# A four-layer mixture-of-experts network on one Trainium2 core: where a pair's last residues and the next pair's input split stand on VectorE

## The reference, cut to what matters

```
x = x + _L0_ffn_ref(_L0_cond_ref(x, cond_8, ...), ...)    # gated MLP chosen per batch, attention over 16 experts
x = x + _L1_ffn_ref(_L1_cond_ref(x, cond_8, ...), ...)
# _L1_ffn_ref, x here is the output h of the conditioned layer:
shared = relu(xt @ sW1 + sb1) @ sW2 + sb2                 # the shared expert, every token
probs = softmax(xt @ router_W + router_b)
top_p, top_i = top_k(probs, 3)                            # 3 of 15 routed experts per token
routed = sum_e cw[n, e] * (relu(xt @ eW1[e] + eb1[e]) @ eW2[e] + eb2[e])
return shared + routed
```

## Time and profile before

| what | value |
|---|---|
| time, median of 3 runs (lowest to highest) | 1533.56 us (1532.3 to 1539.36) |
| the profiled execution: its own time, its span | 1535.98 us, 1534.1 us |
| TensorE busy | 1321.8 us, 86% |
| VectorE, ScalarE, GpSimd busy | 1030.5 us (67%), 591.7 us (39%), 701.5 us (46%) |
| mean granted TensorE clock | 0.898 |
| chain that ended last, by engine | PE 56%, DVE 16%, issue 10%, POOL 9%, ACT 4% |

### The profile page before, as it was taken

How to read it: one execution, slowest core, us unless ns; L and a number is a source line. 1 busy time by engine, 2 the same in 40 slices (tenths; PEclk the granted TensorE clock), 3 DMA queues, 4 the chain that set the end, 5 groups by cost and what they waited for, 6 DMA issues and landing times.

```text
span 1534.1 us, 18711 instructions
## 1 busy us (share of the span) xinstructions
PE 1321.8 (86%) x6536; PEld 1118.3 (73%) x6536; DVE 1030.5 (67%) x1854; ACT 591.7 (39%) x984; POOL 701.5 (46%) x371
## 2 busy tenths in 40 slices
PE   5999989999994799727888999988898979896698
PEld 4898776898782799715776788876687767774587
DVE  8499665499753555526766433498648884789887
ACT  3302422301420588604445455534552445342241
POOL 4320113720015467573002453386656674467790
PEclk9898987898985899958999999999999999996798
DMA  5300001400006699841000332221121222121000
GB/s 197 133 29 14 28 28 55 139 26 3 1 14 226 206 280 310 266 156 55 1 0 21 107 106 89 76 82 63 62 90 55 76 82 85 41 69 47 9 1 28
DMA packets 51773, 128.74 MB, mean 84 GB/s; under 512 B 6353, under 2 KB 30433, under 8 KB 51553
## 3 DMA queue, kind: packets, MB, share of 16 engines
q1 hardware_dynamic: 43840, 109.86, 22.0%
q0 software_dynamic: 4608, 12.59, 2.5%
q10 hardware_dynamic: 3232, 5.11, 0.9%
HBM read 105.25 MB, written 22.28 MB: 83 GB/s over the span
## 4 chain that ended last, share of the span: by engine, by line
PE 56%; DVE 16%; issue 10%; POOL 9%; ACT 4%; DMA 2%; another core or an unknown queue 2%; ACTq 1%; SPq 0%; POOLq 0%; DVEq 0%
PE bank L405 17%; PE bank L408 16%; PE bank L409 16%; POOL VW L458 4%; DVE bank L2335 2%; DVE G L458 1%; PE bank L804 1%; POOL w_lo L593 1%; DVE acc L2359 1%; DVE F L2359 1%; DVE acc L2628 1%; PE bank L953 1%; PE bank L774 1%; ACT w_hi L1601 1%
## 5 line engine op out<-in xcount | busy, mean ns | idle before, releaser
L405 PE MATMUL bank<-x_hi,w_hi 128*128 128x512 f32 (+1 forms) x560 | 221.6, 396 | 38.5 <-POOL w_lo L636 16.3
L636 POOL TENSOR_TENSOR w_lo<-raw,w_hi 128x1024 fp32r<-128x1024 f32 x48 | 117.7, 2453 | 226.5 <-ACT w_hi L1601 211.7
L408 PE MATMUL bank<-x_lo,w_hi 128*128 128x512 f32 (+1 forms) x560 | 215.4, 385 | 0.0
L409 PE MATMUL bank<-x_hi,w_lo 128*128 128x512 f32 (+1 forms) x560 | 214.6, 383 | 0.0
L405 PEld LDWEIGHTS bank<-x_hi,w_hi 128*128 128x128 f32 x560 | 111.8, 200 | 65.6 <-POOL w_lo L636 20.1
L405 PE MATMUL bank<-hid_hi,w_hi 128*128 128x512 f32 x328 | 134.3, 409 | 27.3 <-DVE hid_lo L2290 12.8
L1707 ACT ACTIVATE hid_hi<-bank 128x512 fp32r<-128x512 f32 x96 | 57.4, 598 | 196.4 <-DVE bank L2335 196.4
L409 PE MATMUL bank<-hid_hi,w_lo 128*128 128x512 f32 x328 | 131.8, 402 | 0.0
L408 PE MATMUL bank<-hid_lo,w_hi 128*128 128x512 f32 x328 | 131.8, 402 | 0.0
L409 PEld LDWEIGHTS bank<-x_hi,w_lo 128*128 128x128 f32 x560 | 111.5, 199 | 19.9
L408 PEld LDWEIGHTS bank<-x_lo,w_hi 128*128 128x128 f32 x560 | 111.9, 200 | 18.5
(11 more groups left out here) (473 smaller groups left out, 3643.6 us busy)
## 6 DMA issues: line engine op xcount, KB each, us to landing
raw<-in_skill SPq DMA_DIRECT2D x32, 768.0 KB
raw<-in_shared SPq DMA_DIRECT2D x16, 768.0 KB
raw<-in_l1e SPq DMA_DIRECT2D x20, 513.0 KB
base<-xs SPq DMA_DIRECT2D x38, 256.0 KB, 4.5
ys<-F SPq DMA_DIRECT2D x38, 256.0 KB, 5.0
VW<-in_l1e SPq DMA_DIRECT2D x18, 513.0 KB, 5.2
raw<-in_l0c SPq DMA_DIRECT2D x12, 512.0 KB
raw<-in_qkv SPq DMA_DIRECT2D x8, 768.0 KB
```

What stands on the lines that cost most here:

```text
L405: i = nc.tensor.matmul(out, sh, mh, start=first, stop=False)
L408: nc.tensor.matmul(out, sh, ml, start=False, stop=False)
L409: return nc.tensor.matmul(out, sl, mh, start=False, stop=last)
L636: nc.gpsimd.tensor_tensor(lo[:, UP3], src[:, UP3], hi[:, UP3].bitcast(F32), ALU.subtract).then_inc(w_up_ready.sem, 1)
```

## The change

On VectorE, the four residues of the shared expert stand between `place_rows(0)` and `place_rows(1)`, in both pairs. In pair 0, the split of the next pair's `xT[2]` follows them, and that of `xT[3]` follows `place_rows(1)`; at the head of pair 1 there is no split any more. On TensorE, pair 1 waits for `sh_done` of pair 0 as well, since `x_pair` no longer says that the banks are free.

```
@@ TensorE, head of a pair
                         if cc == 0:
                             pe.wait_ge(*x_pair(it, u + 1))
+                            if it > 0:
+                                pe.wait_ge(*sh_done(it - 1, u + 1))
@@ VectorE
-                def split_x(layer, u):
-                    step(v.tensor_copy(x_hi[u][:], xT[2 * it + u][:]))
-                    v.tensor_tensor(x_lo[u][:], xT[2 * it + u][:], x_hi[u][:].bitcast(F32),
+                def split_x(batch, u):
+                    step(v.tensor_copy(x_hi[u][:], xT[batch + u][:]))
+                    v.tensor_tensor(x_lo[u][:], xT[batch + u][:], x_hi[u][:].bitcast(F32),
                                     ALU.subtract).then_inc(x_pair.sem, 1)

-                dve.wait_ge(*x_in[2 * it](0, 1))
-                split_x(0, 0)
                 if it == 0:
+                    dve.wait_ge(*x_in[0](0, 1))
+                    split_x(0, 0)
                     prepare_gates()
-                dve.wait_ge(*x_in[2 * it + 1](0, 1))
-                split_x(0, 1)
+                    dve.wait_ge(*x_in[1](0, 1))
+                    split_x(0, 1)
@@ the two calls in the middle: split_x(1, u) becomes split_x(2 * it, u)
...
@@ VectorE, end of a pair
                 place_rows(0)
-                place_rows(1)
                 for u in U:
                     for m in range(KD):
                         dve.wait_ge(*sh_hi(it, 2 * u + m + 1))
                         v.tensor_tensor(hid_lo[u][:, m, :], B(u, m)[:], hid_hi[u][:, m, :].bitcast(F32),
                                         ALU.subtract).then_inc(sh_lo.sem, 1)
+                if it == 0:
+                    dve.wait_ge(*x_in[2](0, 1))
+                    split_x(2, 0)
+                place_rows(1)
+                if it == 0:
+                    dve.wait_ge(*x_in[3](0, 1))
+                    split_x(2, 1)
```

More of the change, by code:

```diff
@@ L2024, in _ @@
                     if n == 13:
-                        split_x(1, 0)
+                        split_x(2 * it, 0)
                 projected(1, 0)
@@ L2028, in _ @@
                 wbot_residue(1)
-                split_x(1, 1)
+                split_x(2 * it, 1)
                 RE = slice(1, E1)
```

## The result

The changed kernel takes 1514.95 us (median of 4 runs) beside 1532.93 us for the kernel before (4 runs): a ratio of 0.9898, 95% interval 0.9851 to 0.9945. The same two kernels compared again in two later groups of runs, on chips of their own, gave 0.9924 (0.9896 to 0.9952) and 0.9931 (0.9911 to 0.9951). Taken from the ratios the gain is 10.4 to 15.6 us, by the medians 12.3 to 18.0 us, against 14.7 forecast. One of the four runs of the changed kernel, 1696.72 us with a mean granted TensorE clock of 0.717, is left out of the ratio, as are single runs of 4783.94 and 2529.63 us in the later groups.

The account below looks back on a forecast made before the run. The kernel was taken as bound by TensorE (56% of the chain), with waits on other engines. 4.40 + 3.56 + 1.30 us in pair 0 and 4.40 + 1.08 in pair 1 make 14.74: 1518.8 us, range 1512.5 to 1526.

Parts of the forecast that it names:

- The residues in pair 0: End of pair 0: TensorE's whole stall before the first down matmul goes, 4.40 us.
- named as a sign: In the changed kernel's profile, the stall before the first down matmul is below 0.5 us in both pairs.
- The split and the added wait: Pair 0's end: stall before next pair's first matmul goes, 3.56 us; splits hidden, wait for `sh_done` priced at 0.
- The clock in pair 0: Down straight behind `rank(1)` takes 7.17 us instead of 8.47: 1.30 us less, bounds 0 and 2.97.
- The HAM clock gate: Skill's rule: closing an idle gap leaves the clock high, down takes 5.50 us, sum 3.3 us larger over both pairs.
- The whole stretch from ranks to head: End of pair 0's `rank(1)` to next pair's first matmul: 4.40, 3.56 and 1.30 us less.
- Pair 1: End of pair 1: 4.40 us stall and 1.08 us of down's time gained, 5.48 us passed on through ScalarE's train.
- rival B: Pair 1: delays of ScalarE's copies vanish, falling before the densest DMA traffic; 5.3 us more, 1513.5 us; 11%.
- rival D: ScalarE's zeroing train, pair 1: all seven DMAs go slow, train 14.8 us longer, 1533.6 to 1536 us; 5%.
- Rival A: Pair 1's gain is not passed on, as ScalarE's and SP's zeroing trains overlap; 1524.3 to 1521.9 us; 20%.
- Rival C: Clock terms are 0 or negative, the fall reaching into the next pair's head; 1524.4 to 1521.2 us; 14%.
- The sum: Both pairs: 14.74 us gained, from a median of 1533.56 to 1518.8 us.

Follow-up runs that it names:

- first group: On one chip, against the kernel before: residues alone 1521.52 us, split alone 1530.03, changed kernel with pair 1 in old order 1525.65, changed kernel again 1519.93.
- late scatters: Kernel before plus eight idle GpSimd subtractions between pair 1's last twelve scatters: 1514.69 us, with the kernel before at 1508.47.
- other trains: Kernel before with twelve zeroing DMAs issued from SP and three from ScalarE: 1509.92 us, ratio 1.0004.
- third group: On one chip, ratios to the kernel before: itself 1.0001, changed kernel 0.9931, kernel before with `ZERO_SP = 12` 1.0004, changed kernel with early `rank(0)` 0.9938.
- second and third group: Second: idle GpSimd work in changed kernel 1498.47 us, in kernel before 1514.69; changed kernel with `ZERO_SP = 5` 1498.88, also with early `rank(0)` 1497.4. Third: see its line.

## Why the prediction was right, and where it was not

**The residues in pair 0: right.** Forecast 4.40 us. In the changed kernel's first profile no wait is left, with the residues alone 0.21 us, and in its repeats 0.53 and 0.33 us: a gain of 3.9 to 4.4. 0.53 is just over the 0.5 us that I had named as a sign. I had put VectorE's free moment 4.4 us ahead of the end of `rank(1)`; it was 2.6 us ahead in the first profile and 0.8 us in the one with 0.53.

**The split and the added wait: right.** Forecast 3.56 us hidden; the split alone gave 3.59. Nothing waits for `sh_done`: head follows the bias matmuls without idle in every profile that has the split moved.

**The clock in pair 0: right in the mean, and in three executions of seven.** I took one row, 7.17 us for down. In seven executions with the residues early and `rank(0)` in its old place it took, up to the first transpose, 5.59, 6.86, 8.46, 8.39, 5.57, 7.12 and 7.03 us, a mean of 7.00; in the old order it took 8.26 to 8.31 in five. (The prediction's 8.47 and 7.17 end 0.16 us later, with the last matmul.) The windows of the changed kernel show both levels of the clock (2.4 GHz throughout, then mostly 1.2 GHz):

```profile
221.00:228.00 7.00, 7.00 (x39) 5.79 (x40) 6.52 (x18) 0.18 (x2) 4.01 (x4) 1.00 0.21 75
443.00:452.00 9.00, 9.00 (x29) 7.33 (x30) 7.80 (x25) 0.00 (x0) 5.51 (x6) 0.63 0.41 139
```

TensorE is busy all of the time in both. The rule of the Trainium skill weighed in the prediction ("TensorE: Matmul & The Clock Gate", The HAM clock gate) fits the first and not the second, so neither it nor my row alone could have said 5.6 here and 8.3 there. A closed gap gave back between nothing and 2.7 us of clock.

What I had not looked at is where the clock fell. Stretches of pair 0, one of the changed kernel's first profile and two of its repeat in the first group:

```profile
214.30:217.60 3.30, 3.30 (x10) 2.62 (x10) 2.80 (x16) 0.35 (x1) 0.00 (x0) 0.50 0.00 0
```

```profile
214.00:223.00 9.00, 9.00 (x68) 8.43 (x67) 7.70 (x42) 4.62 (x9) 0.78 (x1) 1.00 0.19 58
223.50:230.00 6.50, 5.97 (x15) 4.67 (x15) 6.05 (x18) 0.00 (x0) 4.66 (x4) 0.50 0.21 76
```

In the first the clock fell in `rank(0)`'s 128x16 matmuls (211.12 to 214.4), the low level lay under `shared_up(1)`, and down ran at the high one. In the second it was high all through `shared_up(1)` and fell at the end of `rank(1)`'s 128x16 matmuls (223.54), so the low level lay under down. Of the seven executions two are of the first kind (5.59 and 5.57 us) and five of the second (6.86 to 8.46). In the kernel before it fell behind both. So part of what down shows as gained or lost is only the low stretch moved by one block; and where `shared_up(1)` ran at the high level, TensorE came to down sooner against VectorE, which fits the waits of 0.21 to 0.53 us that are left in four of those five. My 7.17 us stands for the second kind: with its measure three of the five took 7.02, 7.28 and 7.20 us.

The whole stretch from ranks to head was forecast 9.26 us shorter. It was 21.68 to 21.75 us in four executions of the kernel before (one with late scatters, one with other trains), and 14.14, 14.16, 12.26, 11.86, 11.25 and 11.25 in six of the new order: 7.5 to 10.5 us less, 9.2 in the mean. That the mean meets the forecast is partly luck: the two executions with the clock high throughout down and the two with it low for some 6 us of it lie about as far off on either side.

**Pair 1: the step that failed.** I wrote that "ScalarE's start sets the end" and let 5.48 us through, with the scatters "some 10 us of slack". In the first profile of before the start was indeed on the path. In the changed kernel ScalarE's train starts 10.4 us after the ranks instead of 20.7, 4.40 us of it by the stall and the rest by rival B, the copies' delays, which went; the clock gave nothing (down 8.28 us against 8.25). But then something else ends the stretch. In the changed kernel's first profile it is the last scatter's landing, 2.5 us behind SP's issue train. In its repeat and with the residues alone it is SP's own train, at 0.7 us a step, which SP left without any wait for a DMA. At the quick pace it is the scatters again. The term is 7.7 and 9.7 us between whole kernels at the slow pace, and 2.5 us at the quick one, where 5.48 was forecast; the times of the first group give 5.2 us for it (1.3 to 9.1), in which the forecast lies. The scatters' slack was counted only against the zeroing train (498.2), and that train was slow in this one profile; on the quick chips it was over long before the scatters were. I had the slow steps in a row and used them for rival D alone, as a danger of the change, and not as the reason why the train was on the path at all.

**Rival A** (two trains beside each other lengthen each other) is not borne out. At the slow pace SP's eight DMAs took 10.22, 11.43 and 20.08 us in the new order, where the trains overlap, and 13.72, 13.12 and 21.88 in the old one, where they hardly do: the spread is the pace's and not the overlap's. At the quick pace they took 10.34 us with the overlap and 9.56 without. The rule of the Trainium skill cited there ("Perfetto Trace Analysis", DMA Instruction — HWDGE) would make each of two trains longer by the overlap; the measured 0.8 us says that at the quick pace it hardly shows. That less than 5.48 us is passed on did come true at the quick pace, by the scatters and not by A's way.

**Rival B** came at the slow pace, but not for the reason given, SP's eight DMAs: at the quick pace the kernel before makes both copies at once too, at 472.33, while SP's DMAs run from 465.39. The delays belong to the slow pace. **Rival C** came in pair 0 in two of the six executions of the new order: where down took 8.4 us, 7.5 of the 7.96 us of stalls is all that was gained. Its worst, 3.2 us of loss in the bias matmuls, never came; with down at the high level they took 4.61 us against 4.14. **Rival D** did not come in the changed kernel. With the residues alone ScalarE's seven DMAs took 24.1 us (459.54 to 483.68) against 14.85, and the stretch was 2.6 us shorter than before and not 8 to 10.

**The sum.** Forecast 14.74 us. By stretches it is 15.2 us (7.54 and 7.69) between the first profile of before and the changed kernel of the first group, 11.9 in the third group (9.44 and 2.48), where the times say 0.69% of 1510, 10.4 us, with the interval from 7.4 to 13.4, and the medians 12.3. The median of the first comparison, 18 us, holds some us of chance.

**Left open.** Why the queues go at 0.7 us a step in six profiles (the two first and the first group's) and not in the eight others; whether they do so in executions without a profile is not shown either. The timed ratios on the slow and a quick chip, 0.9924 and 0.9931, do not differ, which speaks against a large effect outside profiles but doesn't settle it; the kernel before takes 1532.8 us on the slow chip and 1508.5 and 1510.0 on the others in time too, and whether the pace has a part in this is not shown. In no group did both paces show, so chip and pace can't be told apart. Why the clock falls in one execution behind `rank(0)` and in another behind `rank(1)` is open too.

## What to carry to other kernels

In a hand-ordered queue, look for an instruction that others wait for and whose inputs are ready, standing behind one that waits: moving it forward is worth the stall's bracket in the timeline (3.59 us for 3.56 here), give or take what the clock does behind it (0 to 2.7 us here), as long as nothing else ends soon after. Where a joint waits for several trains (here zeroing, weight loads, scatters), list when each of them ends before pricing one: shortening the last is worth no more than its distance to the next. And a distance read from one profile may be that chip's or that execution's; look at whether its steps have the length that they have elsewhere.

## What the runs showed that I had not expected

A queue can fall into a pace at which register steps of SP or ScalarE that take 0.02 to 0.15 us elsewhere take 0.70 us each, for 8 us and more with hardly a break (480.4 to 488.8 in the kernel before). The longest register move before a zeroing DMA was 0.038 us or less in each of the eight profiles of the second and third group, and 0.59 to 1.40 us in each of the six others. With `rank(0)` early, all four down stretches took 5.57 or 5.58 us, the high clock throughout, while the clock was at 0.50 from 214 to 220 us, ahead of pair 0's; the kernel gained nothing.
